# First stage of a fused model: step 0 goes through to its router before step 1's keys, scores and values

## The reference

```python
h = _L0_tok_ref(x, conv_w, conv_b, pos_table)
h = concatenate([h, txt], axis=1)                      # [16, 113, 192]
h = h + _L0_attn_ref(_layernorm(h), memory, Wq, bq, Wk, bk, Wv, bv, Wo, bo)
h = h + _L0_ffn_ref(_layernorm(h), scale, gate_w, gate_b, w1, b1, w2, b2)
h = h + _L1_attn_ref(_layernorm(h), ...)
h = h + _L1_ffn_ref(_layernorm(h), ...)
```

## Time and profile before

| | |
|---|---|
| runs, median of 3 | 985.52 us (976.06 to 992.17) |
| profiled execution, own time | 979.58 us |
| its span | 977.8 us |
| mean granted PE clock | 0.855 |
| PE busy | 797.9 us (82%), 4860 matmuls |
| DVE busy | 495.4 us (51%) |
| ACT busy | 306.4 us (31%) |
| POOL busy | 365.4 us (37%), of it 152.8 us in 64 scatter DMAs (L212) and 153.8 us in 64 gather DMAs (L223) |

### The profile page before, as it was taken

How to read it: one execution, slowest core, us unless ns; L and a number is a source line. 1 busy time by engine, 2 the same in 40 slices (tenths; PEclk the granted TensorE clock), 3 DMA queues, 4 the chain that set the end, 5 groups by cost and what they waited for, 6 DMA issues and landing times.

```text
span 977.8 us, 14811 instructions
## 1 busy us (share of the span) xinstructions
PE 797.9 (82%) x4860; PEld 572.6 (59%) x4860; DVE 495.4 (51%) x1223; ACT 306.4 (31%) x571; POOL 365.4 (37%) x233
## 2 busy tenths in 40 slices
PE   7988872279999999988979788779799799888572
PEld 4665662147667777756767574554656656656351
DVE  4354655524644444658676965363824743634210
ACT  1121321023333333333424337144352252342200
POOL 3015888786820287758786100010200100000000
PEclk9787765569999999997979899858789879989795
DMA  8831113334543344444111000000000000000000
GB/s 235 238 106 46 35 29 72 68 79 115 119 124 88 87 117 114 103 127 98 35 29 31 1 1 1 1 1 1 2 0 1 14 0 0 13 3 1 15 0 15
DMA packets 81395, 52.96 MB, mean 54 GB/s; under 512 B 42942, under 2 KB 76719, under 8 KB 80305
## 3 DMA queue, kind: packets, MB, share of 16 engines
q1 hardware_dynamic: 27330, 29.82, 10.9%
q0 software_dynamic: 40960, 11.98, 6.8%
q10 hardware_dynamic: 13040, 10.30, 3.7%
HBM read 29.53 MB, written 21.69 MB: 52 GB/s over the span
## 4 chain that ended last, share of the span: by engine, by line
PE 60%; POOL 16%; DVE 9%; issue 6%; ACT 3%; DMA 3%; SPq 0%; DVEq 0%; ACTq 0%; POOLq 0%
POOL work L223 8%; POOL xs_scratch L212 6%; PE ex_up L1143 6%; PE ex_up L1144 6%; PE ps L2270 4%; PE ps L2201 3%; PE ex_yp L1166 3%; PE ex_yp L1167 3%; PE ps L1355 2%; PE ps L1357 2%; PE ps L1350 2%; PE ps L2210 2%; PE ps L1356 2%; PE a_ps L392 1%; PE ps L1366 1%
## 5 line engine op out<-in xcount | busy, mean ns | idle before, releaser
L223 POOL DMA_INDIRECT work<-ys_scratch,place x64 | 153.8, 2403 | 87.5 <-DMA ys_scratch<-ex_yb 57.5
L212 POOL DMA_INDIRECT xs_scratch<-e_t,e_routed x64 | 152.8, 2387 | 43.0 <-issue 29.3
L1242 DVE TENSOR_SCALAR ex_bb<-ex_up 128x384 f32<-128x384 f32 x44 | 24.5, 558 | 118.6 <-PE ex_up L1144 87.7
L1143 PE MATMUL ex_up<-e_wa,ex_x 128*128 x176 | 75.1, 509 | 8.4 <-issue 6.9
L1144 PE MATMUL ex_up<-e_wb,e_ex_x 65*128 x176 | 73.9, 501 | 0.0
L2480 POOL TENSOR_TENSOR H<-H,f_hh 113x768 f32 (+1 forms) x4 | 7.2, 1810 | 146.7 <-DVE f_hh L2623 146.7
L2458 POOL TENSOR_SCALAR f_veps<-f_mv 113x4 f32<-113x4 f32 x10 | 1.9, 194 | 144.8 <-DVE f_mv L2520 144.8
L1201 ACT ACTIVATE ex_sg<-ex_up 128x384 f32<-128x384 f32 x44 | 21.6, 492 | 106.3 <-PE ex_up L1144 96.9
L2406 ACT ACTIVATE f_pT<-ps 113x452 f32<-113x452 f32 x48 | 26.2, 546 | 77.5 <-PE ps L2210 77.4
L1144 PEld LDWEIGHTS ex_up<-e_wb,e_ex_x 65*128 65x128 f32 x176 | 34.4, 196 | 24.7 <-issue 2.1
L2201 PE MATMUL ps<-f_k,f_q 32*113 32x113 f32 x384 | 32.5, 320 | 16.9 <-DVE f_p L2560 15.8
(11 more groups left out here) (372 smaller groups left out, 1921.9 us busy)
## 6 DMA issues: line engine op xcount, KB each, us to landing
ex_xb<-xs_scratch SPq DMA_DIRECT2D x88, 96.0 KB
ys_scratch<-ex_yb ACTq DMA_DIRECT2D x44, 192.0 KB
xs_scratch<-e_zeros SPq DMA_DIRECT2D x62, 96.0 KB
e_wa<-in_wa SPq DMA_DIRECT2D x4, 1152.0 KB
e_wb<-in_wb SPq DMA_DIRECT2D x4, 576.0 KB
e_wa<-in_patches SPq DMA_DIRECT2D x4, 432.0 KB, 9.3
out<-H SPq DMA_DIRECT2D x4, 339.0 KB
w4a<-in_w4a SPq DMA_DIRECT2D x1, 1216.0 KB
```

The lines of the kernel that those rows point to most:

```text
L212: nc.gpsimd.indirect_dma_start(out=dram.xs, out_offset=bass.IndirectOffsetOnAxis(ap=S.pos[:, j, k:k + 1], axis=0), in_=S.t[:, j, :], in_of ...
L223: nc.gpsimd.indirect_dma_start(out=S.yk[:, it % 2, j, k, :], out_offset=None, in_=dram.ys[it // X.steps], in_offset=bass.IndirectOffsetOnA ...
L1143: mm(o, x1[:, p % 3, t], S.wa[:, bass.ds(w, 2 * I)], start=True, stop=False)
```

## The change

Only the first stage is written anew, and only around steps 0 and 1. On PE, body(0) now goes on with attended(0), one quarter of qk(1), projected(0), two quarters of qk(1), t_transposed(0), the last quarter, and logits(0); body(1) no longer holds those, and ranks(0) stands between the two halves of values(1). DVE and ACT are put in the same order, and POOL sends 7 DMAs of step 0 ahead of root2(1) in place of 5. `qk`, `values` and the `qk_copy` functions are cut so that their tiles can be called one by one. No operation is added or taken away. The diff, its renamings left out:

```diff
             def body(it, first, last):
                 scores(it)
-                values(it)
-                if not first:
+                values(it, 0)
+                if it == 1:
+                    ranks(0)
+                values(it, 1)
+                if it > 1:
                     t_transposed(it - 1)
                 if not last:
                     transposed(it + 1, proj, X1, xn, xn_ok)
                 p_transposed(it)
-                if not first:
+                if it > 1:
                     logits(it - 1)
-                if it == 1:
-                    ranks(0)
+                if first:
+                    attended(0)
+                    qk(1, Q1)
+                    projected(0)
+                    qk(1, Q2, K1)
+                    t_transposed(0)
+                    qk(1, K2)
+                    logits(0)
+                    return
                 if not last:
-                    qk(it + 1)
+                    qk(it + 1, Q1, Q2, K1, K2)
...
                 p_copy(it)
+                if first:
+                    o_copy(0)
+                    q_copy(1)
+                    rows_out(0)
+                    t_copy(0)
+                    k_copy(1)
+                    keep(0)
+                    return
                 if it == 1:
                     later_loads()
                 if not last:
-                    qk_copy(it + 1)
-                if not first:
+                    q_copy(it + 1)
+                    k_copy(it + 1)
+                if it > 1:
                     keep(it - 1)
...
             root1(2)
-            scatter(0, 0, 5)
+            scatter(0, 0, 7)
             root2(1)
             root1(3)
-            scatter(0, 5, 16)
+            scatter(0, 7, 16)
...
             def body(it, first, last):
-                if not first:
+                if it > 1:
                     mean2(it - 1)
-                if not last:
+                if not (last or it == 1):
                     mean1(it + 1)
                 softmax_in(it)
-                if not first:
+                if it == 1:
+                    positions(0)
+                if it > 1:
                     rows_out(it - 1)
                 if not last:
                     norm1(it + 1)
...
-                if it == 1:
-                    positions(0)
+                if first:
+                    o_copy(0)
+                    residual(0)
+                    mean2(0)
+                    q_copy(1)
+                    mean1(2)
+                    k_copy(1)
+                    rows_out(0)
+                    t_copy(0)
+                    top4(0)
+                    chosen(0)
+                    return
```

More of the change, by code:

```diff
@@ L405, in transposed, with qk @@
                     i.then_inc(tiles.filled.sem, 1)
-            def qk(it):
+            def qk(it, *tiles):
                 pe.wait_ge(*proj.copied(it, X1))
                 pe.wait_ge(*proj.copied(it, X2))
[L411 to L434, removed]
+                for n in tiles:
+                    col = w.q if n < K1 else w.k
+                    c0, c1 = (0, LO) if n in (Q1, K1) else (LO, D)
+                    pe.wait_ge(*proj.free(it, n))
+                    o = images(proj.bank(n)[0:c1 - c0, 0:G * NK])
+                    ws = slice(col + c0, col + c1)
+                    mm(o, S.w1h[:, ws], c1h[:], start=True, stop=False)
+                    mm(o, S.w1h[:, ws], c1l[:], start=False, stop=False)
+                    mm(o, S.w1l[:, ws], c1h[:], start=False, stop=False)
+                    mm(o, S.w2hh[:, ws], c2s[:], start=False, stop=False)
+                    mm(o, S.w2l[:, ws], c2s[0:HI, :, :], start=False, stop=True).then_inc(proj.filled.sem, 1)
@@ new lines, in values @@
+            def values(it, h):
+                pe.wait_ge(*proj.free(it, V0 + h))
+                for j in (2 * h, 2 * h + 1):
+                    o = proj.bank(V0 + h)[0:NK, (j % 2) * D:(j % 2 + 1) * D]
+                    ws = slice(w.v, w.v + D)
+                    mm(o, c1h[:, j, :], S.w1h[:, ws], start=True, stop=False)
+                    mm(o, c1l[:, j, :], S.w1h[:, ws], start=False, stop=False)
+                    mm(o, c1h[:, j, :], S.w1l[:, ws], start=False, stop=False)
+                    mm(o, c2s[:, j, :], S.w2hh[:, ws], start=False, stop=False)
+                    m = mm(o, c2s[0:HI, j, :], S.w2l[:, ws], start=False, stop=True)
+                m.then_inc(proj.filled.sem, 1)
@@ L507, in lead @@
                 pe.wait_ge(rest_ok, 5)
-                qk(0)
+                qk(0, Q1, Q2, K1, K2)
                 pe.wait_ge(S.consts_ok, S.n_consts)
@@ L829, in x_low, with q_copy @@
                                  ).then_inc(proj.out(X2), 1)
-            def qk_copy(it):
+            def q_copy(it):
                 dve.wait_ge(*done(att.filled, it, SC - att.filled.per))
@@ L836, in qk_copy, with k_copy @@
                                  ).then_inc(proj.out(Q2), 1)
+            def k_copy(it):
                 dve.wait_ge(*done(proj.filled, it, K1))
@@ L968, in lead @@
                 embedded(3)
-                qk_copy(0)
+                q_copy(0)
+                k_copy(0)
                 dve.wait_ge(S.consts_ok, S.n_consts)
             def body(it, first, last):
-                if not first:
+                if it > 1:
                     mean2(it - 1)
-                if not last:
+                if not (last or it == 1):
                     mean1(it + 1)
                 softmax_in(it)
-                if not first:
+                if it == 1:
+                    positions(0)
+                if it > 1:
                     rows_out(it - 1)
```

6 lines of the change are left out of this document (4 added, 2 removed).

## The result

The changed kernel took **989.69 us** (median of 20 runs, 980.11 to 992.97); the kernel before, measured beside it, 979.46 (20 runs, 967.79 to 992.5). The ratio is **1.0119**, 95% interval 1.0095 to 1.0142: slower by 1.2%, some 12 us.

What follows compares the result with a forecast made beforehand. Root2(2), waiting for mean2(2), was taken to set the end: M 104.4 plus 28.8 gives 133.2, 2.6 us later; weighed two to one against 1.2 earlier, 1.3 us slower on the 985.5 median, so 987 us, range 975 to 997.

Steps and rivals of the forecast that it cites:

- no wait ahead of the ranks: PE's 3.44 us wait for DVE's mask and carry would be gone, covered by step 1's scores and half its values.
- the wait ahead of L522: PE would wait for the router's rows ahead of step 1's transposes: 1.4 us, as a sign 1 to 2 us.
- the wait ahead of step 2's transposes: A new wait of PE, on DVE, which now does positions(0) ahead of norm1(2).
- half clock throughout: The new PE block at half clock, weighed two to one: root2(2) at 133.2, 2.6 us later than before.
- full clock from 46.7 on: Rival: PE at full clock from attended(0) on, root2(2) at 122.2, 8.4 us earlier, 977 us; chance 0.14.
- full clock for good from Q2 and K1 on: Q2 and K1 raise PE's clock and it holds: root2(2) at 129.4, 1.2 us earlier.
- K2: Last of four qk tiles on PE, needing Q1's bank; step 2's was expected at full clock, ending at 96.4.
- takes the place of one removed: PE's 1.4 us wait for the router's rows, counted as replacing PE's removed 3.44 us wait for mask and carry.
- mean2(2) comes 28.8 us after M: DVE's mean2(2), which releases root2(2) on POOL, follows root2(1)'s start by 28.8 us, as in the kernel before.
- M: Start of root2(1) on POOL: 96.8 us in the kernel before, forecast at 104.4.
- My slower rival: Half clock through step 2's K2, attended and projected: root2(2) at 138.4, 7.8 us later, 993 us; chance 0.15.
- meeting: At half clock, step 2's Q1, Q2 and K1 end at 95.2 on PE; ACT's queue frees K2 at 95.1.

Runs made afterwards that it cites:

- Run 8: Changed kernel with load w1w moved forward to step 0, plus step 0's ranks and positions back at their old place: 979.05 us, ratio 1.0013.
- run 5: Changed kernel with only w1w issued early, at the end of step 0's body on ACT, w1g left in place: 977.16 us, ratio 0.9981.
- 7: Changed kernel with the two later loads swapped at their place, w1g before w1w: 974.56 us, ratio 0.9951; measured again 976.62 us, 1.0034.
- changed, loads early: Changed kernel with both later loads, w1w and w1g, issued at the end of step 0's body on ACT: 979.2 us, ratio 1.0012.
- before, loads early: Kernel before with both later loads issued by ACT behind the copy of step 0's attended values: 978.47 us, ratio 1.0009.
- before, held: Kernel before with ACT waiting for step 0's positions before issuing the two later loads: 992.76 us, ratio 1.007.
- changed, late: Changed kernel with both later loads moved to the end of ACT's body(3): 983.06 us, ratio 1.0062.
- before, late: Kernel before with both later loads moved to the end of ACT's body(3): 986.68 us, ratio 1.0144.
- split: Changed kernel with POOL's order put back, 5 scatter DMAs of step 0 ahead of root2(1) and 11 behind: 989.24 us, ratio 1.0128.
- 4: Both later loads issued early, around the end of step 0's work on ACT, in both kernels: ratio 1.0012 changed, 1.0009 before.
- the one with the split at 7: Kernel before with only POOL's part of the change, 7 scatter DMAs ahead of root2(1) and 9 behind: 978.76 us, ratio 1.0014.

## Why the prediction was right or wrong

**Right: the early scatter is not for sale.** The prediction held that root2(2) hangs on mean2(2), that an earlier first scatter buys nothing, and that everything behind root2(2) moves by one amount. Measured: the scatter 3.0 us earlier, root2(2) 9.9 later, the experts 8.9 later, the rest unchanged. Run 8 shows it once more. Of the named signs these were there: the scatter at 79.03 (79 to 84 said), no wait ahead of the ranks, w1g ahead of the Q1 copy, POOL waiting for mean2(1) (8.2 us, where some 3 was said). These were not, or not as said: the wait ahead of L522 is 2.52 us and not 1 to 2; the wait ahead of step 2's transposes is 0.58 us, on ACT and not on DVE; root2(2) comes 34.6 us after root2(1) and not 28 to 29, and POOL waits 6.2 us for mean2(2) where the two were to arrive together.

**The PE block: pieces right, clock in none of my cases.** I had it at half clock throughout, at full clock from 46.7 on, or at full clock for good from Q2 and K1 on. It rose at about 52, so that projected(0) ended at 55.15 and not at 58.2, and it fell again soon behind PE's wait for the router's rows. From there each piece has the length that I gave it at half clock: K2 2.5 us, logits 3.1, scores 5.4, half of the values 3.0, 2.9 from ranks to scatter. So the scatter came 4.0 us before my 83.0, and qk(2) at 83.6, 4.3 before my 87.9. PE's wait that "takes the place of one removed" may thus be dearer than its 2.5 us: the clock stands at full ahead of it and at half behind it. That the wait brought it down is not shown; no run takes this wait away.

The Trainium skill (TensorE: Matmul & The Clock Gate, Part 1) says that sustained matmul activity releases the full clock. Between 47 and 60 us the trace now agrees, in the block for which I gave that rule a small chance; the stretch 120 to 140, 20.00 of 20 us busy at 0.57, again does not.

**Mis-sized: ACT's queue.** I took the 6.44 us of the earlier trace rows as the price of issuing w1g. It measured 9.67, 3.2 more. That ate most of the 4.3 us by which qk(2) was ahead, and it alone made the stall of 2.62 us ahead of K2 that the forecast did not have. What it is follows from runs 5 and 7: w1g's issue is short (0.33) with w1w gone ahead 18 us before, and w1w's is short (0.32) behind w1g; only w1g directly behind w1w is held. The DMA view of run 5 for the stretch 68 to 78 us, when w1w is the only load on the way, shows what kind of transfer that is:

```profile
DMA packets 37, 0.27 MB, mean 27 GB/s; under 512 B 0, under 2 KB 0, under 8 KB 37
q10 hardware_dynamic: 37, 0.27, 6.3%
```

6.3% of 16 engines is one engine, without a pause: at 27 GB/s the 679 KB take some 25 us. w1w has 97 partitions (192 / 2 + 1, with the bias as a last row), w1g has 96. The Trainium skill (DMA: Bandwidth & Descriptors, section "Why a DMA increments its semaphore by 16 and not by 1") says that a DMA is spread over the largest number of engines up to 16 that divides its slowest dimension, which gives one engine for 97 and sixteen for 96; the trace agrees for w1w, and for w1g it shows far more than one engine at work behind its issue (45.5% of 16 for ACT's queue in 83 to 85 us of run 5). That it is the 97th partition which makes w1w slow was not tried by a run. The length of the hold varies with what else is in flight:

| run | w1g's issue, us | scatters running beside it |
|---|---|---|
| before; changed, loads early; before, loads early | 6.44; 6.59; 6.72 | no |
| changed; before, held | 9.67; 8.49 | yes |
| changed, late; before, late | 7.58; 7.35 | yes |

All three without scatters are shorter than all four with. I had carried the figure from a place without them to one with them. The packets of ACT's queue in the DMA views show what is common to all seven: from w1w's issue to the end of the hold, 19 to 23 of them have moved (19 before, 20 in the changed kernel, 23 in the held one).
**Failed: "mean2(2) comes 28.8 us after M".** M itself came out close, 105.88 against 104.4, but by terms that cancel: K2 started 1.2 us earlier than I had it, then took 1.1 us more and attended 1.6 us more, both at half clock where I had full. Root2(2) followed after 34.6 us, and those 5.8 us are the greater part of the miss of 7.3 (140.48 against 133.2). I had read 28.8 off a trace in which part of that stretch ran at full clock, and treated it as a length of work. The runs show it to be a length at a clock. Without a stall ahead of K2 it is 28.8 (loads early), 29.0 (late), 31.0 (w1w early, and swapped in both traces) and 30.3 (ranks late); with one it is 34.6, 35.3 (split, in the longest of its six runs) and 35.3 (held, old order). Of the 3.6 us between the changed kernel and the swapped one, step 2's attended makes 1.7 (3.75 against 2.07 us) and projected, by the starts of its first product and of the scores behind it, 1.8 (133.41 to 138.09 against 127.17 to 130.0), both at half clock against full. My slower rival had the right mechanism, half clock through step 2's K2 and attended, but even it kept the 28.8; it gave 138.4 for root2(2), which measured 140.48.

So the accounting against the swapped kernel, same instructions but for the order of two DMA issues: PE stalls 2.6 us, root2(1) is 4.5 later (105.88 - 101.37), root2(2) 8.1 (140.48 - 132.40), the experts' first product 7.8 (209.17 - 201.35; 8.8 by the second trace), and the ratios to the kernel before are 1.0119 against 0.9951 and 1.0034, some 8 to 16 us. The queue is the cause: it alone in the old order gives 1.007, and without the hold ahead of Q1's copy the new order gives 0.995 to 1.003 (runs 4, 5, 7 and 8). Two thirds of the 8 us, though, come behind the stall, with the clock at half.

**Where my chances stood.** 0.64 went to a case between 2 us faster and 5 slower, 0.15 to one 5 to 8 slower. The forecast had qk(2) and the queue "meeting" within a tenth of a microsecond, at 95.2 and 95.1, and I did not draw from it that any longer hold turns into a bare stall of PE. The issue had one row as its source, at a place with no scatters beside it. Both should have moved weight to the slower case.

**Open.** Why the clock falls behind one stall and not behind another; and how late loads lengthen the last scatter's landing from 8.9 to 14.5 and 15.1 us. The DMA view of the kernel before with late loads, for the stretch 188 to 194 us just ahead of that landing, gives a hint (packets; then the scatters' queue with its share of 16 engines):

```profile
DMA packets 58, 0.01 MB, mean 1 GB/s; under 512 B 57, under 2 KB 57, under 8 KB 58
q0 software_dynamic: 58, 0.01, 2.6%
```

2.6% of 16 is less than half of one engine: nothing but a thin rest of the scatters is on the way, as if it stood on the one engine that w1w had slowed. Against a simple form of this stands that w1w is long done: ACT's queue moves its last packet before 175 us. No run tried it.

## What to carry to other kernels

When pieces are moved, look at each DMA issue that stands ahead of a moved wait on the same queue: its issue can hold the engine when a slow transfer stands directly in front of it, so its price has to be read at the place where it goes, and here it helped to put the slow load last on its queue or a stage earlier. Take as a constant between two events only what ran at one clock; a stall of 2.6 us came with a loss of 8 us here. The load with 97 partitions ran on one DMA engine; whether loading its bias row by itself would mend that was not tried.

## What the runs showed of the hardware that was not expected

- A load of 216 KB takes 0.33 us to issue 18 us behind a load of 679 KB that runs on one DMA engine at 27 GB/s, and 6.4 to 9.7 us directly behind it, which is until 19 to 23 packets of the first have moved; in the other order both take 0.3.
- The same two loads issued at 138 and 142 us, 35 us ahead of it, lengthen the landing of an indirect scatter from 8.9 to 14.5 and 15.1 us; the kernel before with them there took 1.4% longer (0.9 to 2.0).
- The time at which the clock rises differs from one execution to the next: the kernel before and the one with the split at 7 are the same program up to the first scatter, and it stands at 82.02 in one and 79.41 in the other. Over the six profiles of the old order it lies between 79.26 and 91.36 us; with the new one, with the ranks between the halves, seven profiles have it between 78.75 and 79.07.
